# Who splits the shared experts' weights: GpSimd, or the scalar and vector engines

## The reference

```python
x = x + xattn(layernorm(x), ctx)       # a quantised batch product
x = x + moe(layernorm(x))              # the stage of this change
x = x + attention(layernorm(x), ctx)   # 16 heads of 128
x = x + hadamard_ffn(layernorm(x))     # hidden size 2048

def moe(x):                            # x: 2048 tokens x 512
    shared = sum(gelu(x @ Wsh_up[e]) @ Wsh_down[e] for e in range(2))     # 512 -> 256 -> 512
    probs = softmax(x @ W_router)                                         # 16 experts
    top_v, top_i = top_k(probs, 2)
    routed = sum over each token's 2 experts of gate * (gelu(x @ Wrt_up[e]) @ Wrt_down[e])
    return shared + routed
```

## Time and profile before

| | us |
|---|---|
| median of 3 runs | 2259.78 |
| lowest and highest | 2257.94, 2260.43 |
| the profiled execution | 2255.5 |
| its span, first to last instruction | 2253.9 |
| TensorE busy in the span | 1957.6 |
| VectorE busy | 1340.8 |
| ScalarE busy | 816.9 |
| GpSimd busy | 1047.9 |

### The profile page before, as it was taken

How to read it: one execution, slowest core, us unless ns; L and a number is a source line. 1 busy time by engine, 2 the same in 40 slices (tenths; PEclk the granted TensorE clock), 3 DMA queues, 4 the chain that set the end, 5 groups by cost and what they waited for, 6 DMA issues and landing times. The chain is left out here.

```text
span 2253.9 us, 28904 instructions
## 1 busy us (share of the span) xinstructions
PE 1957.6 (87%) x9625; PEld 1614.8 (72%) x9625; DVE 1340.8 (59%) x2075; ACT 816.9 (36%) x1603; POOL 1047.9 (46%) x857
## 2 busy tenths in 40 slices
PE   0349858883499999999999999999987999999999
PEld 0126647772388888888888888888866788888887
DVE  7894448886776666666677666566657333333333
ACT  4212238772244444344444444444432111111111
POOL 2756443224566656666667666666644221022200
PEclk9769979997699999999999999999999999999999
DMA  4043379996365555555555655555542000000002
GB/s 170 0 167 138 102 282 379 364 377 194 99 200 141 165 156 156 170 149 154 165 158 150 167 154 150 171 144 165 147 117 84 29 29 15 15 28 28 0 1 75
DMA packets 163347, 312.97 MB, mean 139 GB/s; under 512 B 15680, under 2 KB 41024, under 8 KB 163264
## 3 DMA queue, kind: packets, MB, share of 16 engines
q1 hardware_dynamic: 145856, 253.18, 36.6%
q0 software_dynamic: 17408, 58.73, 8.1%
HBM read 203.33 MB, written 108.53 MB: 138 GB/s over the span
## 5 line engine op out<-in xcount | busy, mean ns | idle before, releaser
L1260 POOL TENSOR_TENSOR t_pT_lo<-t_pT_raw,t_pT_hi 128x512 fp32r<-128x512 f32 x256 | 327.8, 1300 | 251.0 <-ACT t_pT_hi L1330 249.6
L1421 DVE TENSOR_REDUCE t_sums<-t_score 128x1 f32<-128x512 f32 x256 | 170.9, 690 | 156.6 <-PE t_score L51 156.2
L1728 DVE TENSOR_TENSOR f_lin<-f_lin,f_silu 128x512 f32<-128x512 f32 x64 | 44.7, 700 | 286.5 <-PE f_lin L51 286.5
L1343 ACT ACTIVATE t_probs<-t_score,t_sums 128x512 f32<-128x512 f32 x256 | 175.1, 684 | 79.8 <-DVE t_sums L1421 64.5
L1411 DVE STREAM_TRANSPOSE t_blocks<-t_probs 128x512 f32<-128x512 f32 x256 | 172.7, 694 | 21.2 <-ACT t_probs L1343 21.2
L1403 DVE SCALAR_TENSOR_TENSOR x_res<-t_out,t_sums,x_res 128x512 f32<-128x512 f32 x256 | 179.2, 741 | 3.3 <-PE t_out L51 3.3
L1655 POOL TENSOR_TENSOR f_w_hi<-w_raw,f_zeros 128x1024 fp32r<-128x1024 f32 x16 | 30.4, 1902 | 317.7 <-PE f_gate L51 313.9
L1330 ACT ACTIVATE t_pT_hi<-t_pT_raw 128x512 fp32r<-128x512 f32 x256 | 160.4, 626 | 2.7 <-DMA t_pT_raw<-turned_blocks 2.6
L1688 ACT ACTIVATE f_silu<-f_gate 128x512 f32<-128x512 f32 x64 | 38.3, 598 | 306.5 <-PE f_gate L51 306.5
L51 PE MATMUL t_score<-t_wv_hi,t_cT_lo 128*128 128x256 f32 x512 | 144.9, 283 | 0.0
L51 PE MATMUL t_score<-t_wv_lo,t_cT_hi 128*128 128x256 f32 x512 | 144.9, 283 | 0.0
(11 more groups left out here) (260 smaller groups left out, 6028.4 us busy)
## 6 DMA issues: line engine op xcount, KB each, us to landing
turned_blocks<-t_blocks SPq DMA_DIRECT2D x256, 256.0 KB, 3.8
t_pT_raw<-turned_blocks SPq DMA_DIRECT2D x256, 256.0 KB, 4.1
e_up_raw<-in_L_ffn_Wrt_up_dram SPq DMA_DIRECT2D x47, 512.0 KB, 6.8
e_down_raw<-in_L_ffn_Wrt_down_dram SPq DMA_DIRECT2D x47, 512.0 KB, 6.3
tokens_by_expert<-e_xg SPq DMA_DIRECT2D x1, 12032.0 KB, 39.4
e_xg<-tokens_by_expert SPq DMA_DIRECT2D x47, 256.0 KB, 6.7
outputs_by_expert<-e_y_out SPq DMA_DIRECT2D x47, 256.0 KB, 6.7
wq_raw<-in_L_xattn_Wq_dram POOLq DMA_DIRECT2D x32, 256.0 KB, 4.3
```

Source lines behind the costliest of these rows:

```text
L1260: pool.tensor_tensor(pT_lo[:, q], pT_raw[:, q], f32(pT_hi[:, q]), ALU.subtract).then_inc(p_ready, 1)
L1343: act.activation(probs[:, t % 2, :], score_bank[t][:, :], ACT.Exp, bias=neg_max[:, t:t + 1], accum_out=inv[:, p, t:t + 1]).then_inc(exp_re ...
L1421: dve.tensor_reduce(neg_max[:, t:t + 1], score_bank[t][:, :], AX.X, ALU.max, negate=True).then_inc(max_ready, 1)
L1728: dve.tensor_tensor(lin_bank[k][:, :], lin_bank[k][:, :], silu[:, k, :], ALU.mult).then_inc(mid_done, 1)
```

## The change

ScalarE writes `hi` of the shared experts' weights (a Copy activation) and VectorE subtracts for `lo`, each at new places in their lists. GpSimd no longer splits these weights. It sets its constants right after the router's split, and then waits until all of them are split (`down_ready` at 2) before its first butterfly load. On VectorE the statistics of batch 3 move behind `ln.vector_lo` of batch 1 and the four subtractions. What SP and TensorE do is as before.

```diff
@@ experts_phase, gpsimd
-            zero = zeros[:, :].unsqueeze(2)
-
-            def split_down(n):
-                pool.wait_ge(down_hi_ready, n + 1)
-                pool.tensor_tensor(down_lo[:, n % 2], down_raws[n % RAW_RING], f32(down_hi[:, n % 2]),
-                                   ALU.subtract).then_inc(down_ready, 1)
-
-            for i in range(E_SH):
-                pool.wait_ge(up_in[i], 16)
-                pool.tensor_tensor(up_hi[:, i], up_raw[:, i], zero.to_broadcast([P, KD, DE]),
-                                   ALU.add).then_inc(up_hi_ready, 1)
-                pool.wait_ge(up_hi_ready, i + 1)
-                pool.tensor_tensor(up_lo[:, i], up_raw[:, i], f32(up_hi[:, i]), ALU.subtract).then_inc(up_ready, 1)
-                pool.wait_ge(down_in[i], 16)
-                pool.tensor_tensor(down_hi[:, i], down_raw[:, i], zero[:, 0:KE].to_broadcast([P, KE, D]),
-                                   ALU.add).then_inc(down_hi_ready, 1)
-                split_down(i)
-
             for e in range(E_RT):
                 pool.memset(rank[:, :, e:e + 1], float(E_RT - e)).then_inc(const_ready, 1)
...
+            pool.wait_ge(down_ready, E_SH)
+
             def butterfly_load(c):
@@ scalar
+            def shared_up_hi(i):
+                act.wait_ge(up_in[i], 16)
+                act.activation(up_hi[:, i], up_raw[:, i], ACT.Copy).then_inc(up_hi_ready, 1)
+
+            def shared_down_hi(i):
+                act.wait_ge(down_in[i], 16)
+                act.activation(down_hi[:, i], down_raw[:, i], ACT.Copy).then_inc(down_hi_ready, 1)
+
+            shared_up_hi(0)
             turned_hi(0)
+            shared_up_hi(1)
             logitsT_out(0)
             turned_hi(1)
+            shared_down_hi(0)
             logits_out(0)
+            shared_down_hi(1)
             logitsT_out(1)
             unit(0)
@@ vector
+            def shared_up_lo(i):
+                dve.wait_ge(up_hi_ready, i + 1)
+                dve.tensor_tensor(up_lo[:, i], up_raw[:, i], f32(up_hi[:, i]), ALU.subtract).then_inc(up_ready, 1)
+
+            def shared_down_lo(i):
+                dve.wait_ge(down_hi_ready, i + 1)
+                dve.tensor_tensor(down_lo[:, i], down_raw[:, i], f32(down_hi[:, i]), ALU.subtract).then_inc(down_ready, 1)
+
             ln.vector_lo(dve, 0, xT_hi, xT_lo, 0)
+            shared_up_lo(0)
+            ln.vector_lo(dve, 1, xT_hi, xT_lo, 1)
+            shared_up_lo(1)
+            shared_down_lo(0)
+            shared_down_lo(1)
             stats.compute(dve, B - 1)
-            ln.vector_lo(dve, 1, xT_hi, xT_lo, 1)
             ln.vector_norm(dve, 2, 2)
             ln.vector_norm(dve, 3, 3)
             low(0)
```

## The result

The changed kernel takes 2253.97 us (median of 20 executions, 2250.54 to 2259.41) against 2259.78 (20 executions, 2254.66 to 2267.76). The ratio is 0.9975 with a 95% interval of 0.9966 to 0.9984: 5.6 us faster, 3.6 to 7.7. The range held it. But the likeliest case, 1.7 us, is not what happened: what happened is nearest to the first rival, to which I gave 0.20.

What follows compares the result with a forecast made beforehand. GpSimd's splits hold VectorE's statistics, for which TensorE waits. Of 8 to 10 us won at up(1), normalising under butterflies gives back about 4 to 6 and the clock 2.4, leaving 1.7: 2258.1 us, range 2252.0 to 2261.5.

Steps and rivals of the forecast that it cites:

- the likeliest case: Whole kernel: butterflies hold normalising and TensorE's clock drops before down(0), leaving 1.7 us won, 2258.1 us; chance 0.45.
- the first rival: Normalising: butterflies do not hold the tiles; down(0) 9.9 us earlier, choose loses 2.7, net 7.2, 2252.6 us; chance 0.20.
- Part 1: Head of ScalarE's list: shared_up_hi(0) waits for its weight ahead of turned_hi(0), so route(0) loses 3.1 us, to 152.7.
- Part 2: TensorE's 11.83 us wait goes: route(1) starts at 161.5 and up(1) ends 8 to 10 us earlier.
- Part 3: VectorE's new list: subtractions end at 164.4 (down_ready), statistics at 170.5, undisturbed normalising at 174.2.
- Part 4: Butterflies from 171.3, 6.8 us after load issue, hold six normalising tiles; down(0) at 181.65, 4.1 us won.
- The price of a held tile: VectorE's normalising beside butterflies: tiles get in at butterfly ends, each lengthening the next by 0.18; six take 9.0 us.
- the sum: All terms together: 4.1 us won at down(0), 2.4 lost to the clock, 1.7 left, giving 2258.1 us.
- Part 5: TensorE idle before down(0) until 181.65, so its clock falls to half, costing 2.4 of the 4.1 us.
- full blocking both ways: VectorE and GpSimd ports: each engine blocks the other for its whole instruction; 0.3 us won, 2259.5 us; chance 0.07.
- Part 6: Rest of the stage: fourth chunk ends at 241.2, choose begins at 244.4, still clear of one another.
- The signs of being wrong: Profile: first butterfly after 174, eight tiles under 5 us, or a changed distance from down(0) to the slots.

Runs made afterwards that it cites:

- order_only: The kernel before with only VectorE's statistics of batch 3 moved behind the lo of batch 1, GpSimd keeping its eight splits; ratio 0.9956.
- split_only: The changed kernel with the statistics of batch 3 put back before the lo of batch 1; only splits and GpSimd's wait moved; ratio 0.9980.
- turned_first: The changed kernel with ScalarE's first weight copy behind turned_hi(0) instead of ahead of it; ratio 0.9960.
- before_again: The kernel before, unchanged, for a second profile; slots 126.6 us after the stage's start.
- after_third: The changed kernel, unchanged, profiled again beside the probe of late additions; 2258.03 us for the one profiled run.
- late_chunk: order_only plus GpSimd's fourth butterfly chunk after VectorE's choice, attention's first loads ahead of it, fifth chunk loaded after the scatters; ratio 0.9941, median 2238.45 us.
- no_pool_wait: The changed kernel without GpSimd's wait for down_ready before its first butterfly load; ratio 0.9973.
- adds_first_2: The changed kernel with GpSimd waiting for all dense-part additions before its first scatter, second run of this probe; 2274.18 us for the one profiled run.
- early_load: The changed kernel with GpSimd's first butterfly load issued ahead of the wait for the split weights; ratio 1.0008.

## Why the prediction was right or wrong

- **What bounds the stage: right.** The splits on GpSimd held VectorE's statistics, and TensorE waited for VectorE. Either part of the change ends that (order_only, split_only).
- **Part 1, head of ScalarE's list, 3.1 us: right.** `route(0)` at 153.02 for a forecast of 152.7; with `turned_hi(0)` first (turned_first) the slots come 2.7 us earlier. So this part of the change is a loss inside one that wins.
- **Part 2, `route(1)` at 161.5: right** (161.77), and TensorE ran it at full clock (granted 1.00 from 160 on).
- **Part 3, `down_ready` at 164.4 and statistics to 170.5: right** (164.7 and 170.6).
- **Part 4 failed, at "So the butterflies begin at 171.3".** The load took 8.3 us from issue to first butterfly, not 6.8 (165.10 to 173.36). The term that was mis-sized is this load, by 1.4 us, with 0.6 us more from its issue. As only three microseconds of normalising lay behind 171.3, it decided nearly all: one tile was held instead of six. The moment of the issue does not explain it. In the kernel before and in the change the load was issued at nearly the same time (before_again, then after_third):

```profile
166.48 0.86 POOL L648 DMA_DIRECT2D e_w2a<-in_L_ffn_W_dram  x1
173.39 1.29 POOL L657 TENSOR_TENSOR e_w2b<-e_w2a 128x512 f32<-128x512 f32 x1 [6.06 <-DMA e_w2a<-in_L_ffn_W_dram]
```

```profile
166.32 0.86 POOL L632 DMA_DIRECT2D e_w2a<-in_L_ffn_W_dram  x1 [17.88 <-DVE e_down_lo L891]
174.59 1.66 POOL L641 TENSOR_TENSOR e_w2b<-e_w2a 128x512 f32<-128x512 f32 x1 [7.41 <-DMA e_w2a<-in_L_ffn_W_dram]
```

In all four profiles in which GpSimd does the splits up to shortly before the issue (two of before, order_only, late_chunk) it took 6.7 to 6.9 us. In all eight in which GpSimd had waited 15 to 18 us for `down_ready` it took 8.2 to 8.4, and in no_pool_wait 7.0. All transfers together move 410 GB/s then in either kind (166 to 168 in these two profiles). So the row of the kernel before, "the same load under the same fill took 6.8", was no row for the kernel after, and it was my one argument against the first rival, which needed less than the 3 us that I asked of it. Why the load takes longer there, no run shows.
- **The price of a held tile: right, for one and for two of them.** In the change one tile is held, and the eight take 4.72 us instead of 3.74, 0.98 more. In adds_first_2, where the first butterfly comes 2.69 us behind the first tile, two are held, 1.95 more (VectorE, then GpSimd):

```profile
170.10 5.69 DVE L171 TENSOR_SCALAR e_ln_xn<-x_res,mean_var,rstd 128x512 f32<-128x512 f32 x8
```

```profile
172.79 1.29 POOL L641 TENSOR_TENSOR e_w2b<-e_w2a 128x512 f32<-128x512 f32 x1 [7.31 <-DMA e_w2a<-in_L_ffn_W_dram]
174.05 1.46 POOL L642 TENSOR_TENSOR e_w2b<-e_w2a 128x512 f32<-128x512 f32 x1
```

The sum had 9.0 us for six held tiles, which is 1.04 more for each. Six in a row were held in no run.
- **The clock of Part 5: right as a mechanism,** as early_load shows: 5.38 us idle, then half clock. In the change it did not come about. That `down(0)` came at 181.53 there, for 181.65 in the sum, is a coincidence: it was the statistics that were held, and no tile.
- **The page's rule on the ports.** The Trainium skill (SBUF — State Buffer, section "Who interferes with whom") has the other engine blocked for the whole instruction. For VectorE behind GpSimd the trace agrees: the held tile of the change took 1.52 us instead of 0.54, for it was done only after the butterfly had ended. For GpSimd behind VectorE it agrees in part. The first butterfly, issued 0.03 us behind the seventh tile, took 1.66 us, 0.37 longer than 1.29, near the rest of that tile. The second, in front of which the held tile got in, took 1.47, 0.18 longer, where a tile by spacing takes 0.46; in adds_first_2 it was 1.46. So the 0.18 of the sum held. In `choose` steps of 0.42 lengthened a butterfly by 0.03 to 0.15. With full blocking both ways a held tile would have cost 1.27 by the sum's working, which is an estimate from that section; it cost 0.98.
- **Part 6, `choose` still clear of the fourth chunk: right only for the sum's case.** The rival had it: `choose` at 237.1 lies in the chunk. It costs 2.9 us (forecast 2.7).
- **The rival's sum:** 9.9 - 2.7 = 7.2 forecast. Measured from the stage's start: 9.3 - 2.9 = 6.4, slots 6.6. Over the three profiles it is 8.8 - 2.9 = 5.9, slots 5.9, and the total is 5.6 with 7.7 at the interval's end.
- **The signs of being wrong.** Two of the three named came: the eight tiles took under 5 us (4.72), and from `down(0)` to the slots it was 86.2 us instead of 83.5. The first butterfly came at 173.36, before 174, and yet the tiles were all but through. So the range held because it was wide enough to take in the rival, and not because the sum was right.
- **"A microsecond at `down(0)` should appear in the total": true for the slots rather**, since `choose` stands between, and within the intervals of seven kernels of eight. In the one profile of the change it was hidden behind late additions, which no row of the kernel before had shown.

## What to carry to other kernels

Before moving work off an engine that holds another by a shared port, try to move the held work out of its time: here two swapped lines gave as much as the whole change or more. When a term of the sum is the duration of a transfer, ask whether the change alters what the issuing engine does before it: here the same load took 6.8 us behind a busy GpSimd and 8.3 behind a waiting one. Where the outcomes on both sides of such a term differ by several microseconds, give both like chances. And when a stage moves forward, look for what lies over its new place: the background work of GpSimd that was harmless over matmuls cost 3 to 5 us when `choose` slid under it, and putting it behind `choose` brought the slots 3.4 and 4.6 us forward.

## What the runs showed of the hardware that was not expected

- The first 512 KB load of W2 took 6.7 to 6.9 us from issue to first butterfly in all four profiles in which GpSimd had worked up to shortly before the issue, and 8.2 to 8.4 in all eight in which it had waited 15 to 18 us, with 410 GB/s moved in all. The cause is open.
- VectorE's additions, one PSUM input and one SBUF input, were 3 to 13 us late beside indirect scatters in eight of twelve profiles, where 1.4 us apart is usual, and never before the first scatter.
- A GpSimd transfer that was next in its list at 147.3 was issued only at 151.74 (early_load; in no_pool_wait 148.35 and 152.52), with no wait in the program; the profile puts these 4 us down to "issue".
- `TENSOR_REDUCE` kept its 0.42 us beside butterflies while `TENSOR_TENSOR` with both inputs in SBUF went from 0.42 to as much as 1.37, and once to 1.51 (split_only).
